# Spreading the block inverse's series over four quarters of TensorE's array in a gated delta rule kernel

## What is computed

```python
def step(S, inp):
    qt, kt, vt, gt, bt = inp
    S = S * jnp.exp(gt)[:, None, None]
    kv = jnp.einsum('hk,hkv->hv', kt, S)
    delta = (vt - kv) * bt[:, None]
    S = S + kt[:, :, None] * delta[:, None, :]
    o = jnp.einsum('hk,hkv->hv', qt, S)
    return (S, o)
...
x = x + _L0_attn_ref(xn, ...) + _L0_ffn_ref(xn, ...)
xn = _layernorm(x, axis=-1)
x = x + _L1_attn_ref(xn, ...) + _L1_ffn_ref(xn, ...)
```

## Time and profile before

| | before |
|---|---|
| median of 3 runs | 2869.35 us (2865.93 to 2870.66) |
| profiled execution, its own time | 2868.26 us |
| its span, first to last instruction | 2866.6 us |
| TensorE busy | 2700.8 us, 94% of the span |
| VectorE busy | 2196.3 us, 77% |
| ScalarE busy | 1823.8 us, 64% |
| GpSimd busy | 1534.7 us, 54% |
| mean granted TensorE clock | 0.98 of full speed |

### The profile page before, as it was taken

One profiled execution on the slowest core, in us unless ns is written; L12 is line 12 of the kernel. 1 busy time (PEld: TensorE's weight loads), 2 busy tenths in 40 slices (PEclk: granted clock), 3 DMA queues, 4 the chain that ended last, 5 costly groups with the idle time before them and its releaser, 6 DMA issues. The chain is left out here.

```text
span 2866.6 us, 75659 instructions
## 1 busy us (share of the span) xinstructions
PE 2700.8 (94%) x24303; PEld 1879.6 (66%) x24303; DVE 2196.3 (77%) x4677; ACT 1823.8 (64%) x6310; POOL 1534.7 (54%) x3737
## 2 busy tenths in 40 slices
PE   5999679999999999999999999999999999869998
PEld 4556357776777776776777667767766776645555
DVE  3443468888888888888888888888888888637775
ACT  3322467777777777777777777777777776323332
POOL 1000277666777666776766677776667776210000
PEclk9999889999999999999999999999999999969999
DMA  4000121222222222223222222222222222010000
GB/s 93 0 1 0 27 53 37 56 44 54 43 49 40 51 50 48 51 42 52 37 53 46 55 41 50 41 48 46 54 46 47 53 37 46 18 44 1 8 8 15
DMA packets 485567, 113.69 MB, mean 40 GB/s; under 512 B 423296, under 2 KB 484336, under 8 KB 485168
## 3 DMA queue, kind: packets, MB, share of 16 engines
q1 hardware_dynamic: 485168, 108.76, 19.1%
HBM read 80.63 MB, written 28.06 MB: 38 GB/s over the span
## 5 line engine op out<-in xcount | busy, mean ns | idle before, releaser
L548 POOL TENSOR_TENSOR Tb<-Tb,btmp 64x14 f32<-64x14 f32 (+6 forms) x896 | 369.1, 412 | 71.9 <-issue 1.7
L544 POOL TENSOR_TENSOR btmp<-Bk,Tb 64x14 f32<-64x14 f32 (+6 forms) x896 | 353.6, 395 | 60.6 <-POOL Tb L536 0.2
L1231 DVE SCALAR_TENSOR_TENSOR S<-S,gs,bank 128x128 f32<-128x128 f32 x1024 | 287.2, 342 | 46.8 <-PE bank L787 28.2
L933 ACT ACTIVATE oq<-bank,gs 128x128 f32<-128x128 f32 x512 | 160.2, 364 | 241.2 <-PE bank L624 241.2
L1127 DVE SCALAR_TENSOR_TENSOR R<-bank,gs,xn 128x128 f32<-128x128 f32 x512 | 155.8, 346 | 183.2 <-PE bank L613 183.1
L1262 DVE SCALAR_TENSOR_TENSOR conv<-raw,ckq,conv 128x512 f32<-128x512 f32 x384 | 284.7, 755 | 14.5 <-ACT conv L1016 7.4
L1262 DVE SCALAR_TENSOR_TENSOR conv<-raw,cv,conv 128x512 f32<-128x512 f32 x384 | 282.3, 749 | 8.6 <-ACT conv L1016 1.5
L759 PE MATMUL bank<-wz_h,xnT 128*128 128x256 f32 x1024 | 263.5, 380 | 0.0
L743 PE MATMUL bank<-xnT,wkq 128*128 128x512 f32 x512 | 241.2, 614 | 10.6 <-POOL mkX L429 10.6
L832 PE MATMUL bank<-wout_h,gT 128*128 128x256 f32 x1024 | 246.4, 384 | 0.1
L1014 ACT ACTIVATE raw<-bank 128x512 f32<-128x512 f32 x256 | 154.0, 601 | 144.9 <-PE bank L743 144.9
(11 more groups left out here) (354 smaller groups left out, 6704.2 us busy)
## 6 DMA issues: line engine op xcount, KB each, us to landing
rowb<-decay_rows SPq DMA_DIRECT2D x256, 64.0 KB, 4.0
blk_n<-N SPq DMA_DIRECT2D x256, 64.0 KB, 2.2
Tp<-blk_t SPq DMA_DIRECT2D x128, 128.0 KB, 2.9
Wp<-blk_w SPq DMA_DIRECT2D x128, 128.0 KB, 3.0
wkq<-in_L_attn_W_qkvz_dram SPq DMA_DIRECT2D x32, 128.0 KB, 2.2
wv<-in_L_attn_W_qkvz_dram SPq DMA_DIRECT2D x16, 256.0 KB, 2.6
Bk<-blk_n SPq DMA_DIRECT2D x64, 64.0 KB, 2.6
blk_t<-Tb SPq DMA_DIRECT2D x64, 64.0 KB, 2.6
```

Of the source, the lines that this page charges most:

```text
L544: pool.tensor_tensor(tmp, Bk[:, j, j + 1:].unsqueeze(2).broadcast_to([64, 15 - j, j]), Tb[:, j, 0:j].unsqueeze(1).broadcast_to([64, 15 - j ...
L548: pool.tensor_tensor(Tb[:, j + 1:, 0:j], Tb[:, j + 1:, 0:j], tmp, ALU.subtract).then_inc(row_rdy, 1)
L933: i = act.activation(oq[t.c % 2][:, u, :], pQS[:, v], ACT.Copy, scale=gs[t.c][:, GAM, u:u + 1])
L1231: i = dve.scalar_tensor_tensor(out=S[:, 2 * b + v, :], in0=S[:, 2 * b + v, :], scalar=gs[t.c][:, kind, 2 * h + v:2 * h + v + 1], in1=pKU[b ...
```

## The change

The series' four products are spread over all four quarters. Value head 0 of a pair stays on the diagonal quarters. Value head 1 goes to the off-diagonal ones: its rows are in one half of the partitions and its result lands in the other ("turned"). For that `x16` makes value head 1's X twice, turned (`pX`) and at home (`pXh`), twelve products in place of eight; `xev_home` is one more VectorE operation; and `Wp` holds value head 1's W twice, at home and turned, which `base_out` loads with six DMAs in place of two. The series' two PSUM banks become one tensor `series` over both. The gram products (`causal`) lose bank 5 and go to bank 2, so they and the transposes that share bank 2 wait for one another. Several lists are written in another order, on TensorE, ScalarE, VectorE and GpSimd. Two waits of the last head's tail are changed too.

```diff
-        Wp = [sb(f"Wp{r}", [P, 2, U, 64]) for r in range(2)]
+        Wp = [sb(f"Wp{r}", [P, 3, 2, 2, 64]) for r in range(2)]
+        TURNED, W_V0, W_V1 = range(3)
...
+        Xs = sb("Xs", [P, 2, 2, 64])
+        Xh = sb("Xh", [P, 2, 64])
+        Wk = [sb(f"Wk{r}", [P, 2, 2, 64]) for r in range(2)]
...
+        series = ctx.enter_context(nc.psum_tensor("series", [P, 2, 512], F32))
+        bank = [series[:, i - 4] if i in (4, 5) else ctx.enter_context(nc.psum_tensor(f"bank{i}", [P, 512], F32))
+                for i in range(8)]
+        bU = [b[:, :].rearrange("p (u n) -> p u n", u=U) for b in bank]
+        bB = [b[:, :].rearrange("p (b n) -> p b n", b=B) for b in bank]
+        pX, pXh, pW = (series[:, :, P * q:P * q + P].rearrange("p j (s n) -> p j s n", s=2) for q in range(3))
+        pGram = bank[2][:, 0:256].rearrange("p (s j n) -> p s j n", s=2, j=2)
...
-                        sp.dma_start(Wp[r][half[b]].rearrange("p c u n -> p (c u) n"),
-                                     matrices(wd, 0, 2 * U, b)).then_inc(w_in, 16)
+                        sp.dma_start(Wp[r][half[b], W_V0].rearrange("p c s n -> p (c s) n"), of_v(wd, b, 0, 4)).then_inc(w_in, 16)
+                        sp.dma_start(Wp[r][half[b], W_V1].rearrange("p c s n -> p (c s) n"), of_v(wd, b, 1, 4)).then_inc(w_in, 16)
+                        sp.dma_start(Wp[r][half[1 - b], TURNED].rearrange("p c s n -> p (c s) n"), of_v(wd, b, 1, 4)).then_inc(w_in, 16)
...
-                    for j in range(1, 5):
+                    for j in range(1, 3):
                         base_row(t, j)
...
-                    for j in range(5, 11):
+                    for j in range(3, 11):
...
-                    for j in range(11, ROWS + 1):
+                    for j in range(11, 13):
+                        base_row(t, j)
+
+                def base_last(s):
+
+                    t = s.back(S_F + 3)
+                    if not t.live or t.c % 2:
+                        return
+                    for j in range(13, ROWS + 1):
...
                     out_scale(s)
+                    base_last(s)
...
+                    for j in range(2):
+                        for b in range(B):
+                            p, u = half[b], 2 * j
+                            pe.matmul(pX[p, 0, j], Nt[p, u, :], T[p, u, :], start=True, stop=True)
+                            pe.matmul(pX[half[1 - b], 1, j], Nt[p, u + 1, :], T[p, u + 1, :], start=True, stop=True)
+                    for j in range(2):
+                        for p in half:
+                            u = 2 * j + 1
+                            i = pe.matmul(pXh[p, 0, j], Nt[p, u, :], T[p, u, :], start=True, stop=True)
                     i.then_inc(x16_mm, 1)
...
+                    wait(pe, xh_rdy, done)
+                    for j in range(2):
+                        for b in range(B):
+                            p, q = half[b], half[1 - b]
+                            pe.matmul(pW[p, 0, j], Xs[p, 0, j, :], W[p, W_V0, j, :], start=True, stop=True)
+                            i = pe.matmul(pW[p, 1, j], Xs[q, 1, j, :], W[q, TURNED, j, :], start=True, stop=True)
                     i.then_inc(w1_mm, 1)
...
-                    for u in range(U):
-                        for h in half:
-                            i = pe.matmul(pX[h, u], Xs[h, u, :], Wk[0][h, u, :], start=True, stop=True)
+                    for j in range(2):
+                        for b in range(B):
+                            p, q = half[b], half[1 - b]
+                            pe.matmul(pX[p, 1, j], Xs[p, 0, j, :], Wk[0][p, 0, j, :], start=True, stop=True)
+                            i = pe.matmul(pX[q, 0, j], Xh[p, j, :], Wk[0][p, 1, j, :], start=True, stop=True)
                     i.then_inc(w2_mm, 1)
...
-                    for u in range(U):
-                        for h in half:
-                            i = pe.matmul(pW[h, u], Xs[h, u, :], Wk[1][h, u, :], start=True, stop=True)
+                    for j in range(2):
+                        for b in range(B):
+                            p, q = half[b], half[1 - b]
+                            pe.matmul(pW[p, 0, j], Xs[p, 0, j, :], Wk[1][p, 1, j, :], start=True, stop=True)
+                            i = pe.matmul(pW[p, 1, j], Xs[q, 1, j, :], Wk[1][q, 0, j, :], start=True, stop=True)
                     i.then_inc(w3_mm, 1)
...
+                    pe.wait_ge(kd_rdy, t.done())
+                    pe.wait_ge(ssq_rdy, t.done())
                     for h in range(2):
                         for b in range(B):
-                            i = pe.matmul(bank[5][half[b], P * h:P * h + P], y[:, 0, quarter(t, h), b, :], y[:, :, quarter(t, h), b, :],
+                            i = pe.matmul(bank[2][half[b], P * h:P * h + P], y[:, 0, quarter(t, h), b, :], y[:, :, quarter(t, h), b, :],
...
                     queries(s, 0)
-                    causal(s)
                     x16(s)
                     solve(s, 0)
...
                     keys(s, 1)
                     queries(s, 1)
+                    causal(s)
                     w2(s)
                     solve(s, 1)
                     attend(s, 0)
                     w3(s)
                     increment(s, 1)
                     values(s)
+                    gated_tp(s)
                     zproj(s, 0)
-                    gated_tp(s)
                     zproj(s, 1)
...
                     expo(s)
+                    squares(s)
                     evac(s, 0)
-                    squares(s)
+                    evac(s, 1)
                     from_state(s, 1)
-                    evac(s, 1)
                     normed(s)
+                    gtev(s)
                     vscale(s)
-                    gtev(s)
                     ztanh(s)
...
+                def xev_home(s):
+
+                    t = s.back(S_L)
+                    if not t.live:
+                        return
+                    dve.wait_ge(x16_mm, t.done())
+                    wait(dve, w2_mm, t.done(1))
+                    dve.tensor_tensor(Xh[:], pXh[:, 0], mkP[:].unsqueeze(1).broadcast_to([P, 2, 64]), ALU.mult
+                                      ).then_inc(xh_rdy, 1)
...
                     xev16(s)
+                    xev_home(s)
                     uscale(s, 0)
                     gate(s)
                     add_w1(s)
+                    output(s)
                     update(s, 0)
-                    output(s)
                     silu(s)
+                    tap(s, 0, (2,))
+                    rhs(s, 1)
                     strict(s)
-                    rhs(s, 1)
-                    attention(s)
                     add_w2(s)
                     uscale(s, 1)
-                    tap(s, 0, (2,))
+                    attention(s)
                     add_w3(s)
```

More of the change, by code:

```diff
@@ L350, in base_out @@
                         return
-                    rows, made, before, sent, solved = (held(sp, v) for v in (
-                        t.pairs(ROWS, ROWS), t.pairs(1, 1), t.pairs(32), t.pairs(16, 16), t.at(1, -2)))
+                    rows, made, before, w_before, sent, solved = (held(sp, v) for v in (
+                        t.pairs(ROWS, ROWS), t.pairs(1, 1), t.pairs(32), t.pairs(96), t.pairs(16, 16), t.at(1, -2)))
                     r = t.c // 2 % 2
@@ L691, in front_tp @@
                     wait(pe, kd_rdy, t.done(1))
+                    wait(pe, attn_rdy, t.done(1))
                     wait(pe, gT_rdy, t.done(S_E + 1 - S_F))
```

40 lines of the change are left out of this document (17 added, 23 removed).

## The result

The changed kernel takes 3113.37 us (median of 4 runs, 3112.33 to 3116.54), the kernel before 2868.8 (4 runs, 2865.93 to 2870.66): a ratio of 1.0855, 95% interval 1.0837 to 1.0874. It is slower by 244.6 us, about 3.8 for each of the 64 pairs. Its profiled execution has a span of 3108.8; TensorE is busy 2703.6 us of it, 87% in place of 94%.

The account below looks back on a forecast made before the run. TensorE was taken to bound the recurrence (busy 1184.39 of 1200 us). With late loads a pair would take 35.35 against 33.33 us; 62 x 2.0 = 125 us on 2868 gives 2993, rounded to 2990, range 2880 to 3070.

Parts of the forecast that it names:

- both waits: TensorE, next step: about 2.6 us at `w1` for the last W load, then 1 us or less before `gated_tp`.
- Four quarters halve a product: Series products on TensorE: 16 records from 0.52 to 0.26 us; `w1` to `w3` save 0.72 us a step.
- The rival of a floor of 32 ns a record: Series products: record pace is the floor, so `w1` to `w3` save nothing; about 3050 us, chance 0.12.
- VectorE and ScalarE make 0.62 of wait at `solve`, so the finishing step takes 16.3: Finishing step: `solve` on the second half gets its input 0.62 us late; 15.68 + 0.62 = 16.3 us.
- Tb sent at 11.0: GpSimd, finishing step: rows 13 and 14 behind `out_scale` send Tb at 11.0 us in place of 8.20.
- Six loads in 4.1: SyncE's queue: six Wp loads at 0.68 us each take 4.1 us to issue.
- base start to gated_tp 6.1: GpSimd's base blocks start at 25.1; 2.36 us to `out_scale`, at most 3.79 more to `gated_tp`: 31.2.
- gated_tp to the end 4.6: TensorE: behind `gated_tp` stand 3.75 us and the first `zproj`, 0.87, ending the pair at 35.8.
- `Tp` follows 2.69 later: SyncE's queue: `Tp` is loaded 2.69 us after Tb is sent, as in the kernel before.
- With the low ends it is 34.4. I take 35.1: Pair of steps: terms gave 35.8 us, their low ends 34.4; 35.1 was taken, against 32.8 before.
- 0.25 for the weights: Wait for new heads' weights, 0.5 us a pair before: half kept, giving 35.35 against 33.33 a pair.
- the ring keeps its reserve: Rival: Tb leaves at 8.5, W lands at 19 as `w1` wants it, Bk lands early; 2830 us, chance 0.17.

Follow-up runs that it names:

- after_dump: The changed kernel with `dump` issued between the sending of Wb and the loading of Tp: 3028.5 us.
- after_shift: The changed kernel with 32 identity products on TensorE once, ahead of its loop, to move the later instruction loads: 3071.6 us.
- pool_back: The changed kernel with GpSimd's order of before (rows 11 to 14 and the copy to Wb ahead of `out_scale`), six Wp loads kept: 3027.2 us.
- after_fill: The changed kernel with seven identity products of 128 columns ahead of `w1` in every starting step, filling TensorE's wait: 3100.2 us.
- four_loads: The changed kernel with Wp loaded by four DMAs in place of six, nothing else: 3027.7 us.

## Why the prediction was right, and where it failed

The direction, the place of both waits and their order were right; the size was not: 125 us forecast, 245 measured, and 3113 lies above the range's 3070.

1. *Four quarters halve a product:* shown. From the start of a group to the start of the next (medians, unstalled steps), `w2` goes from 0.52 to 0.28, `w1` and `w3` from 0.56 to 0.39, `x16` stays (0.52, 0.51). The saving is 0.58 a step where I had 0.72, and `xev_home` costs 0.17 at `w1` (0.44 to 0.61 between `attend` and it), not 0.25. The rival of a floor of 32 ns a record is out: sixteen start in 0.25 us, where the group took 0.52. The Trainium skill's floor of about 25 ns from start to start (TensorE: Matmul & The Clock Gate, "Wait — 56ns, not 53.3ns?") would ask for 0.40; the measurement differs (0.28) and decides, for records on different quarters.
2. *VectorE and ScalarE make 0.62 of wait at `solve`, so the finishing step takes 16.3:* not by themselves. Where GpSimd's base rows end in time (after_dump) `solve` waits in 12 steps only, 6.1 us in 1200, and the step takes 15.91 (median). In the changed kernel it takes 16.84, since GpSimd's late base rows delay ScalarE and with it VectorE (the chain shown above). With that `w1` is wanted later than 18.9, and its wait is 1.9, not 2.6.
3. *Tb sent at 11.0:* 10.88, but by luck. The sum had `out_scale` wait for the squares and begin at 6.8, take 2.2, and rows 13 and 14 take 2.0. By the medians it begins at 7.83 and in 35 of 41 pairs without an idle moment before it, since rows 11 and 12 end only then, not at 5.75; it takes 1.93, and the rows 1.13. Three errors cancel. *Six loads in 4.1:* 3.98. *dump to Bk 2.82:* 2.84. *Bk to base start 2.85:* 2.68. *base start to gated_tp 6.1:* 6.36. *gated_tp to the end 4.6:* 4.53. These held.
4. **"`Tp` follows 2.69 later" failed.** It follows 4.42 later. Net of shorter steps next to it, it makes `gated_tp` late by 1.34 (32.54 against 31.2). I had taken the landing of Tb as a constant, from one pair of a kernel in which nothing crossed it. With the landing back at 2.5 us (after_shift) the kernel is 42 us faster.
5. **"With the low ends it is 34.4. I take 35.1" failed.** My own terms gave 35.8; with the 1.3 of point 4 they give 37.1, the 37.07 of the table. Of the low ends only that of rows 13 and 14 came (1.13), and the late start of `out_scale` took it back. That choice is 0.7 us a pair, 43 us of the miss.
6. *0.25 for the weights:* the mean of the same pairs is 37.07 as well (the kernel before: 33.37 against 32.81), so nothing. This pulls the other way by some 15 us.

By pairs, 4 to 6 make 37.07 - 35.35 = 1.7 us, 107 of the 120 us between forecast and result. Of the rest, some lies in the last pairs: over the last three `x16` falls back by 15.9 us against the kernel before, 5.3 a pair where the mean has 3.7. I didn't look into the cause. The fall of the clock, which I had not foreseen, is worth some 16 us in this kernel, a small part of it.

The two waits were as forecast, with the path through `Bk` longer than that through `w1` by 1.0 (measured 1.0 in the pairs at full clock). The case "the ring keeps its reserve" would have needed Tb at 8.5; pool_back has it at 8.38 and W in time at `w1` (19.37), and still takes 3027. I had named the `Bk` that must land early only in passing: it was what decided, and `dump`, which the change doesn't touch, stood ahead of it.

## What to carry to other kernels

When one engine is 99% busy, look at what it feeds through a ring before making it faster: here 0.4 us a step of TensorE work was really saved, and had no taker, since a list of GpSimd's that runs unbroken for 28 of the pair's 33 us set the time of `gated_tp`. Count each DMA of a queue by its issue (0.65 us here, for 64 and for 128 KB) and put the issues that wait for nothing into the gaps where the queue waits for a landing; that order was worth 91 us. Look behind a stretch at the lower clock for the next wait: with one there it cost 0.5 us a time, without one 1.7. Look at the pairs one by one before you read a median: two kinds of pairs can stand on either side of it. Where the sum of your own terms gives a value, don't move off it toward its kind end.

## What the runs showed of the hardware

- A copy of 64 KB in 64-byte packets (Tb) landed in 2.5 us when no instruction load ran beside its packets, and in 4.3 when one did (medians of 9 and 55 sends of the changed kernel). In after_shift the 9 that were still crossed landed in 3.0. 32 instructions more at the start of the program moved the crossings and changed the whole time by 42 us (1.3%), with the same work otherwise.
- Sixteen records of 64 columns on four 64x64 quarters start within 0.25 us; from that group to the next it takes 0.28, where on two quarters it took 0.52.
- In the rows of SyncE's queue one issue takes 0.57 to 0.62 us for 64 KB, and two take 1.26 to 1.50 for 128 KB each and 1.25 for 64 KB each.
- After TensorE's wait of 1.9 us at `w1` the granted clock fell to its lower level (1.2 GHz) in about half of the pairs; where the projection ran in it, it took up to 5.40 us, not 3.70. In after_shift there are as many such stretches (43) as in the changed kernel, and it is 42 us faster; in after_fill 9, and it is 13 faster. four_loads has 8 and pool_back 39, and they take the same time (3027.7 and 3027.2).
